# The first loads and the first TensorE products of a cross-attention kernel, rearranged

## The reference, cut to what matters

```python
x = x + xattn(layernorm(x), ctx, ctx, Wq, bq, Wk, bk, Wv, bv, Wo, bo)
x = x + ffn(layernorm(x), W_in, b_in, W_out, b_out)

# xattn: q, k, v = projections; k and v padded from 1601 to 2048 rows
qf, kf = rfft(qt), rfft(kt)
corr = irfft(qf.real * kf.real - 1j * qf.imag * kf.imag)
weights, delay = top_k(mean(corr, heads and channels), 15)
out = sum_k softmax(weights)[k] * v shifted by delay[k];  return out @ Wo + bo
```

## Time and profile before

| | us |
|---|---|
| median of 3 runs | 165.79 |
| lowest, highest | 165.48, 166.21 |
| the profiled execution, its own time | 165.92 |
| its span, first to last instruction | 163.8 |
| TensorE busy in the span | 154.5 |
| VectorE busy | 126.1 |
| ScalarE busy | 111.3 |
| GpSimd busy | 40.4 |

### The profile page before, as it was taken

The page is one execution under the profiler, slowest core; times in us unless marked ns, Lnnn a source line. Parts: engine busy times, 40 slices in busy tenths (PEclk is TensorE's granted clock), DMA queues, the critical chain, the costliest instruction groups (busy, mean ns, idle before and its releaser), DMA issues.

```text
span 163.8 us, 2952 instructions
## 1 busy us (share of the span) xinstructions
PE 154.5 (94%) x1126; PEld 112.5 (69%) x1129; DVE 126.1 (77%) x269; ACT 111.3 (68%) x179; POOL 40.4 (25%) x43
## 2 busy tenths in 40 slices
PE   7999999999999999999999789999999789999990
PEld 5898476787666888996658564444445468888880
DVE  0007879999588759446999879999877799999963
ACT  3265512979862556464489979998889399999900
POOL 8002210008600073000059600199000033320000
PEclk9999999999999999999999999999999999999999
DMA  5999999400000000000000000000000000003306
GB/s 148 264 318 399 403 355 394 139 4 2 4 0 0 0 4 0 0 0 4 0 2 0 0 4 0 0 0 0 4 0 0 0 0 4 0 0 128 133 0 256
DMA packets 6284, 12.16 MB, mean 74 GB/s; under 512 B 576, under 2 KB 3904, under 8 KB 6016
## 3 DMA queue, kind: packets, MB, share of 16 engines
q1 hardware_dynamic: 6272, 11.99, 21.4%
HBM read 9.89 MB, written 2.10 MB: 73 GB/s over the span
## 4 chain that ended last, share of the span: by engine, by line
PE 84%; DVE 8%; ACT 5%; issue 1%; DVEq 0%; POOL 0%; POOLq 0%
PE ps L1256 15%; PE ps L1042 9%; PE ps L1021 9%; PE ps L1231 8%; PE ps L1226 8%; PE ps L999 5%; PE ps L1033 4%; PE ps L1164 4%; PE ps L986 4%; PE ps L1178 3%; PE ps L1074 2%; PE ps L1173 2%; DVE sm L849 2%; DVE sm L932 1%; PE ps L1085 1%; ACT arena L634 1%
## 5 line engine op out<-in xcount | busy, mean ns | idle before, releaser
L1256 PE MATMUL ps<-woutq,arena 128*128 128x256 f16 x256 | 28.7, 273 | 1.3 <-ACT arena L634 0.7
L1256 PEld LDWEIGHTS ps<-woutq,arena 128*128 128x128 f16 x256 | 24.7, 98 | 5.3 <-ACT arena L634 1.5
L619 ACT ACTIVATE arena<-ps,colv,sm 128x512 f32<-128x512 f32 x32 | 23.9, 777 | 2.3 <-PE ps L1231 0.5
L953 DVE SCALAR_TENSOR_TENSOR arena<-scr,sm,arena 128x1024 f16<-128x1024 int16 x16 | 21.3, 1372 | 0.0
L932 DVE TENSOR_REDUCE sm<-arena 128x1 f32<-128x1024 f32 (+1 forms) x17 | 18.9, 1148 | 2.5 <-ACT arena L619 2.5
L1231 PE MATMUL ps<-arena,winq 128*128 128x512 bf16 x64 | 18.6, 379 | 0.1
L1226 PE MATMUL ps<-arena,winq 128*128 128x512 bf16 x61 | 17.9, 379 | 0.3 <-DVE arena L897 0.3
L634 ACT ACTIVATE arena<-arena,sm 128x1024 f16<-128x1024 f32 x15 | 16.4, 1134 | 0.0
L1042 PE MATMUL ps<-wvo,arena 128*128 128x256 f32 x64 | 15.9, 389 | 0.0
L986 PE MATMUL ps<-ones 128*128 128x256 bf16 x96 | 14.1, 303 | 1.0 <-POOL ones L375 1.0
L1021 PE MATMUL ps<-arena,wqk 128*128 128x512 f32 x32 | 14.4, 598 | 0.0
(11 more groups left out here) (201 smaller groups left out, 283.1 us busy)
## 6 DMA issues: line engine op xcount, KB each, us to landing
arena<-x_dram SPq DMA_DIRECT2D x4, 512.0 KB, 9.5
out_dram<-arena SPq DMA_DIRECT2D x8, 256.0 KB, 2.1
arena<-ctx_in_dram SPq DMA_DIRECT2D x4, 448.0 KB, 6.0
tabs<-tab_dram SPq DMA_DIRECT2D x1, 1264.5 KB, 14.1
arena<-winT_dram SPq DMA_DIRECT2D x1, 1024.0 KB, 15.6
arena<-turn_dram SPq DMA_DIRECT2D x1, 1024.0 KB, 11.7
arena<-wout_dram SPq DMA_DIRECT2D x1, 1024.0 KB, 12.4
arena<-wqT_dram SPq DMA_DIRECT2D x1, 256.0 KB, 7.8
```

The source lines that it names most:

```text
L619: a.activation(H[:, f, 512 * c:512 * c + 512], bank("M1", n), ACT.Gelu, bias=colv[:, 6 + f:7 + f], scale=sc1[:, f:f + 1]).then_inc(S["h_re ...
L953: v.scalar_tensor_tensor(out=part, in0=scr16[:, n % 4, :], scalar=rf[:, f:f + 1], in1=piece(Hhi, n), op0=ALU.mult, op1=ALU.subtract).then_ ...
L1256: return t.matmul(o[k // 2][:, 256 * (k % 2):256 * (k % 2) + 256], part[:, t0:t0 + 128], woutq[:, f, :], start=start, stop=stop)
```

## The change

The table `F` is no longer issued by SyncE but by ScalarE, as the first thing in its block. SyncE begins with the first quarter of the context, as two loads of two blocks each (512 columns, 2 KB of every partition in place of 4 KB), with a semaphore for each. The other three quarters, and all that follows on SyncE, stay as they were. TensorE's first fillers are 12 in place of 20. The first two context units are computed together: both banks are taken, then the products of the first half for both channel halves, then those of the second half. The products themselves are the same 32, and units 2 to 7 are unchanged.

```diff
+        ld_first = [sem(f"ld_first{i}") for i in range(2)]
...
             n0, n1 = at["F"][1], at["IN0"][1]
-            sp.dma_start(tabs[:, 0:n0], tab[:, 0:n0]).then_inc(S["ld_F"], 16)
-            for i in range(4):
+            for i in range(2):
+                sp.dma_start(cx[0:AP, 512 * i:512 * i + 512], ctx_in[0][:, 512 * i:512 * i + 512]).then_inc(ld_first[i], 16)
+            for i in range(1, 4):
                 sp.dma_start(cx[0:AP, 1024 * i:1024 * i + 1024], ctx_in[i]).then_inc(ld_ctx[i], 16)
...
+            act.dma_start(tabs[:, 0:at["F"][1]], tab[:, 0:at["F"][1]]).then_inc(S["ld_F"], 16)
             act.wait_ge(S["pool_const"], 1)
             a.activation(warm[:, 0:1], one, ACT.Sqrt)
...
-            keep_clock(0, 20)
+            keep_clock(0, 12)
             pe.wait_ge(S["ld_F"], 16)
-            for i in range(8):
+            def context(o, h, b):
+                return t.matmul(o[:, 128 * (b % 4):128 * (b % 4) + 128], cx[0:AP, 256 * b + 128 * h:256 * b + 128 * h + 128],
+                                F[0:AP, :], start=True, stop=True)
+
+            o = [take_bank(pe, "CD", h) for h in range(2)]
+            for part in range(2):
+                pe.wait_ge(ld_first[part], 16)
+                for h in range(2):
+                    for b in (2 * part, 2 * part + 1):
+                        last = context(o[h], h, b)
+                    if part == 1:
+                        done(last)
+            for i in range(2, 8):
                 bq, h = i // 2, i % 2
                 if h == 0:
                     pe.wait_ge(ld_ctx[bq], 16)
                 o = take_bank(pe, "CD", i)
-                for k in range(4):
-                    b = 4 * bq + k
-                    last = t.matmul(o[:, 128 * k:128 * k + 128], cx[0:AP, 256 * b + 128 * h:256 * b + 128 * h + 128],
-                                    F[0:AP, :], start=True, stop=True)
+                for b in range(4 * bq, 4 * bq + 4):
+                    last = context(o, h, b)
                 done(last)
```

## The result

The changed kernel takes 166.38 us (median of 10 runs, 165.68 to 167.28) against 165.72 for the kernel before (10 runs, 165.27 to 166.21). The ratio is 1.0041, with a 95% interval of 1.0025 to 1.0057. The forecast was 165.15, with 166.1 as the upper end. The profiled execution took 166.12 us with a span of 164.1, so the 2.0 us outside the span are as before; the loss is in the span.

A forecast was written before the change was run, and what follows sets the result against it. TensorE alone was taken to bound the kernel from 0.98 to 33.5 us. Fillers -0.89, wait at unit 4 +0.2 and first half 0 gave -0.7 us, so 165.15 us, range 164.6 to 166.1.

The forecast's parts named there:

- Eight fillers less: TensorE's start: context begins at 3.65 us, clock's rise to 2.4 GHz stays put, so eight fillers less gain 0.89 us.
- The first half ready at 3.65: First context load on SyncE: lands at 3.2 to 3.5 us (bounds 2.5 to 4.6), in time for TensorE, costing 0.
- F from ScalarE: Load of table F at the start: lands at 2.8 us, ahead of 3.65; the move saves one issue, 0.38 us.
- The pause costs half of its length: TensorE waiting for the first half: at most 1.0 us at the lower clock level, costing 0.5 us.
- Rival C: A pause at 3.65 puts off TensorE's clock rise, each us costing 0.5; 167.1 at 4 us delay; chance 0.10.
- Rival B: Context start: late first half or F and later quarters bring waits of 0.5 + 0.7 us, giving 166.1; chance 0.10.
- Rival A: Context stage: with an earlier clock rise loads decide and the fillers were hidden, gain 0 to 0.29, 165.6; chance 0.26.
- The next loads 0.1 earlier, unit 4 waits 0.2: Later context quarters land 0.1 us earlier; unit 4, needed at 8.83, waits 0.2 us for its quarter at 9.0.
- The gain lives on to the end: After the context stage: VectorE's fourth `weighted` waits 0.97 us for TensorE and can start earlier, so the gain reaches the end.

The follow-up runs named there:

- e5: Changed kernel with the first half's eight instructions reading a tile of ones, the loads waited for only behind them: 164.99 us, ratio 0.9954 to the kernel before.
- e10: Changed kernel with 14 fillers in place of 12: 165.42 us, ratio 0.9988 to the kernel before.
- e6: Kernel before with F issued by ScalarE and nothing else changed: 165.62 us, ratio 1.0001.
- e1: Changed kernel with F issued by SyncE again, ahead of the two halves, 12 fillers: 166.41 us, ratio 1.0041 to the kernel before.
- e15: The changed kernel timed once more, without any edit: 166.03 us, ratio 1.0009 to the kernel before.
- e4: Kernel before with 12 fillers in place of 20 and nothing else changed: 167.14 us, ratio 1.0056.
- e9: Changed kernel with F first on SyncE, then the first quarter as four loads of one block, 12 fillers: 166.48 us, ratio 1.0041 to the kernel before.
- e14: Kernel before with 9 first fillers, a wait for GpSimd's memset, then three fp32 products of ones: 167.16 us, ratio 1.0084.
- e3: Changed kernel with 16 fillers in place of 12: 165.42 us, ratio 0.9985 to the kernel before.
- e16: Changed kernel with 16 fillers in place of 12, timed a second time: 165.22 us, ratio 0.9978 to the kernel before.
- e13: Kernel before with its first fillers as 12, a wait for GpSimd's memset, and 6 more: 165.85 us, ratio 1.0006.
- e11: Changed kernel with 16 fillers, the last four behind the wait for F and the first half: 165.65 us, ratio 0.9991 to the kernel before.
- e7: Changed kernel with F first on SyncE, then the two halves, and 16 fillers: 166.17 us, ratio 1.0009 to the kernel before.

## Why the prediction was wrong, by its own steps

Two steps failed together: the landings that were taken as ahead of 3.65 us, which put a pause there, and the price of that pause, which left the rise at 6.75.

- *Eight fillers less, -0.89 us.* The price fits (e5: -0.86, 164.99 against 165.85 for the kernel before on the same chip), but it holds only if TensorE doesn't stand. The step said "as long as the engine stays busy" and took that as given.
- *The first half ready at 3.65, taken at 3.2 to 3.5.* This step failed. It landed at 4.1, within the bounds of 2.5 to 4.6 that were written down but far from the value taken. The working went by bytes over the rate of the first windows. The runs show that halving the half again saves hardly anything: 3.0 us for 112 KB, 2.7 and 3.1 for 224 KB, and 3.4 with the half first of all and `F` beside it. The nearest row was the whole quarter's 3.9, not `F`'s 1.8.
- *F from ScalarE, taken at 2.8.* It landed at 4.4, outside the bounds given (up to 3.8). `F` at the head of SyncE's queue takes 1.8 to 2.0; from ScalarE, beside a large load, it takes 3.5 to 4.7 (e10, e6). The prediction added 0.3 us for the neighbour, and it was 1.9. The rule of the Trainium skill that the loads of all issuers run on the same 16 DMA engines and interleave (DMA: Bandwidth & Descriptors, "Issuing engines are not separate DMA queues") agrees with this; the prediction took from it only the one issue saved. That the small load gave up its place ahead of the large one is the likely reason, and no run tests it alone. e1 shows that `F` wasn't decisive: with `F` there at 2.6, the pause was still 0.63.
- *The pause costs half of its length, 0.5 at most.* This is the step by which the sign turned. It priced the time lost at the lower level and left the moment of the rise in its place. Rival C had the mechanism, at a chance of 0.10, and sized it: 1.4 us of delay eat the gain. The profiled execution has a delay of 1.4 (8.10 for 6.69), the one of e15 3.3. With both terms the sum comes out: -0.89 + 0.37 (half of 0.73) + 0.70 (half of the delay) = +0.2 us, where the end of the context stage moved by +0.30. The same sum gives +1.1 for e15, +1.15 for e4 and +4.0 for e9's profiled execution, measured +1.17, +1.25 and +4.2. It is within 0.15 us for all eight profiled executions with a pause of 0.6 us or more but e14, where 0.3 us more were lost.
- *Rival B* (waits in place of fillers, rise unmoved) would have given 166.1 by waits of 1.2 us; measured are 0.73 in all, and the quarters for units 4 and 6 weren't later. It doesn't hold.
- *Rival A* shows in e5 and e3, where the context is bound by the quarter for unit 2 (not 4, as was worked out).
- *The next loads 0.1 earlier, unit 4 waits 0.2.* The quarters for units 4 and 6 landed 0.7 and 0.8 earlier, the one for unit 2 0.1 later, in the one execution each. No wait at unit 4.
- *The gain lives on to the end.* Right for whatever sign: e16's stage ends 0.97 earlier (12.32 for 13.29), and its span is 1.0 shorter (162.8). VectorE's fourth `weighted` waited 0.97 us for TensorE in the changed kernel, as before, since TensorE wasn't earlier.

What stays open: how long a pause may be. 0.31 us does nothing to the median (e13), 0.95 costs 0.76%, and at 0.66 to 0.73 the runs spread over 2.5 us and more (e11, e15). Also why four of e15's twelve runs of the changed kernel lie by 165, and none of its first ten, which go from 165.68 to 167.28: that may be chance or the chip. And no run here shows the rise in the executions that weren't profiled; that low and high times go with early and late rises is argued from the profiled ones, of which the slowest (e9, 169.88) has the latest rise.

## What to carry to other kernels

Filler products that keep TensorE busy until the first load lands aren't waste to be cut to the expected landing; they have to reach past the latest landing of what is waited for. A wait of 0.7 us ahead of the rise of the clock cost this kernel more than eight fillers. And read the spread of the runs with the median: of the 22 executions of the changed kernel four were near the forecast, eleven in between, and seven at 166.9 and above, which one median doesn't tell.

## What the runs showed of the hardware that was not expected

- The moment of the rise differs between executions of one kernel: 3.95 (e3) and 5.58 (e16) with 16 fillers, 8.10 and 10.01 (e15) for the changed kernel. The Trainium skill (TensorE: Matmul & The Clock Gate, Part 1) says that it varies from run to run, and the traces agree.
- Of the loads second in SyncE's queue, 112 KB took 3.0 us (e9), 224 KB 2.7 and 3.1 (e7, e1), 448 KB 3.9: below 224 KB a smaller load gained next to nothing. The 64 KB of `F` took 1.8 at the head of the queue, and 3.5 to 4.7 from a second queue beside a large load.
- The clock column of the profile stood at 1.00 in stretches where an instruction took twice as long as later. The record behind it begins with the rise (6.69 us before, 8.10 after), so the column can't be used for the first microseconds.
